# One unread fp32 product of 256 columns on TensorE in every part of an attention step that leaves the shared bank unused

## What is computed

```
q_h = exp_map(split(x @ W_q.T)); k_h = exp_map(split(x @ W_k.T)); v_h = exp_map(split(x @ W_v.T))
dist = arccosh(max(1 + 2c * |q - k|^2 / ((1 - c|q|^2) * (1 - c|k|^2)), 1 + EPS)) / sqrt(c)
weights = softmax(-beta * dist - bias)
x = x + (log_map(exp_map(weights @ v_tan)) joined) @ W_o.T
x = x + fp8_gemm(layernorm(x), kernel) + bias
```

## Time and profile before

| | |
|---|---|
| median of 3 runs | 2432.06 us (2428.98 to 2432.98) |
| the profiled execution | 2433.24 us |
| its span, first to last instruction | 2431.4 us |
| ScalarE busy | 1937.7 us, 80% |
| TensorE busy, matmuls | 1945.1 us, 80% |
| VectorE, GpSimd busy | 970.8 us, 362.6 us |
| mean granted TensorE clock | 0.809 of 2.4 GHz |

### The profile page before, as it was taken

How to read it: one execution, slowest core, us unless ns; L and a number is a source line. 1 busy time by engine, 2 the same in 40 slices (tenths; PEclk the granted TensorE clock), 3 DMA queues, 4 the chain that set the end, 5 groups by cost and what they waited for, 6 DMA issues and landing times. The chain is left out here.

```text
span 2431.4 us, 29241 instructions
## 1 busy us (share of the span) xinstructions
PE 1945.1 (80%) x10317; PEld 624.6 (26%) x10317; DVE 970.8 (40%) x2289; ACT 1937.7 (80%) x1184; POOL 362.6 (15%) x223
## 2 busy tenths in 40 slices
PE   4458897989888768888879489798979888888682
PEld 2222232323222222222323123232323222222221
DVE  4432344343534345343444534443343534221413
ACT  1039999998989659998989389899988989999491
POOL 1111121121212002020212102121121212010011
PEclk9959798988888778897989579898888888876675
DMA  1120101001010200202020020201001010200000
GB/s 37 57 57 10 49 10 51 25 19 58 18 58 1 66 9 11 65 1 75 1 66 10 1 75 1 66 10 66 10 18 58 18 49 1 66 1 18 1 18 10
DMA packets 79154, 75.58 MB, mean 31 GB/s; under 512 B 34651, under 2 KB 60508, under 8 KB 78940
## 3 DMA queue, kind: packets, MB, share of 16 engines
q1 hardware_dynamic: 78940, 73.02, 9.6%
HBM read 17.96 MB, written 55.05 MB: 30 GB/s over the span
## 5 line engine op out<-in xcount | busy, mean ns | idle before, releaser
L911 ACT ACTIVATE U<-ps 128x2048 f32<-128x2048 f32 x500 | 939.0, 1878 | 178.6 <-PE ps L820 169.3
L916 ACT ACTIVATE U<-U,sc 128x2048 f32<-128x2048 f32 x512 | 1025.4, 2003 | 0.0
L820 PE MATMUL ps<-q_T,k_T 18*128 18x512 f32 x4096 | 750.4, 770 | 222.7 <-ACT U L911 149.2
L833 PE MATMUL ps<-U,vals 128*32 128x512 f32 x4096 | 680.6, 743 | 50.1 <-ACT U L916 29.1
L820 PEld LDWEIGHTS ps<-q_T,k_T 18*128 18x128 f32 x4096 | 224.5, 218 | 756.0 <-ACT U L911 592.5
L340 PE MATMUL ps<-wT,xnT 128*128 128x384 f32 x512 | 231.7, 581 | 13.7 <-DVE qkv L370 9.4
L370 DVE COPY qkv<-ps 128x384 f32<-128x384 f32 x128 | 71.4, 558 | 342.4 <-PE ps L340 334.8
L306 POOL TENSOR_TENSOR sqr<-qkv 128x768 f32<-128x768 f32 x64 | 94.1, 1470 | 732.4 <-DVE qkv L370 651.2
L833 PEld LDWEIGHTS ps<-U,vals 128*32 128x32 f32 x4096 | 87.9, 118 | 327.7 <-ACT U L916 216.6
L348 PE MATMUL ps<-ident,rows 128*128 128x128 f32 x512 | 99.2, 325 | 84.6 <-POOL rows L323 66.6
L340 PEld LDWEIGHTS ps<-wT,xnT 128*128 128x128 f32 x512 | 98.3, 213 | 161.5 <-issue 107.2
(11 more groups left out here) (174 smaller groups left out, 1336.3 us busy)
## 6 DMA issues: line engine op xcount, KB each, us to landing
q_scratch<-q_T SPq DMA_DIRECT2D x16, 1024.0 KB, 4.5
k_scratch<-k_T SPq DMA_DIRECT2D x16, 1024.0 KB, 6.9
v_scratch<-vals SPq DMA_DIRECT2D x16, 768.0 KB, 10.9
xt<-in_L_attn_x_dram SPq DMA_DIRECT2D x16, 512.0 KB, 3.8
fi_xt<-in_L_attn_x_dram SPq DMA_DIRECT2D x16, 512.0 KB, 4.7
out_dram<-fi_x SPq DMA_DIRECT2D x16, 512.0 KB, 3.2
rk_scratch<-rk SPq DMA_DIRECT2D x16, 32.0 KB, 12.2
wraw<-in_L_attn_W_q_dram SPq DMA_DIRECT2D x1, 256.0 KB, 2.9
```

The lines of the kernel that those rows point to most:

```text
L820: ins = pe.matmul(g.ps[:, 2 * pair + i, :], a.k_T[HB * h:HB * h + RD, b % 2, hg, kt * P:(kt + 1) * P], a.q_T[HB * h:HB * h + RD, G % 3, hg ...
L833: ins = pe.matmul(g.ps[HB * h:HB * h + VW, 6, :], a.vals[:, b % 2, kt, (hg * HPG + h) // 2, DH * (h % 2):DH * (h % 2) + VW], U[:, n % RING ...
L911: act.activation(U[:, n % RING].rearrange("p b n -> p (b n)"), chunk(n), ACT.Ln, scale=-2.0 / EPS, bias=1.0).then_inc(ln_done, 1)
L916: act.activation(U[:, n % RING], U[:, n % RING], ACT.Exp, scale=g.NEGB).then_inc(exp_done, 1)
```

## The change

The step is written as a loop over its two halves. A half without a use of the shared bank now issues `keep_busy`: a wait until VectorE has copied out all uses so far, and one fp32 product of the identity (stationary) with 256 columns of `woT`, into bank 7. Nothing reads it, it raises no semaphore, and the next use overwrites it. There are 576 such halves among 1024: 121 of half 0 and 455 of half 1.

```diff
+                def keep_busy(used):
+
+                    pe.wait_ge(a.b7_copied, used)
+                    pe.matmul(g.ps[:, 7, 0:D], g.ident[:, :], g.woT[:, 0, :], start=True, stop=True)
+
...
                 for n in range(N):
                     G, s = n // STEPS, n % STEPS
+                    used = first_use[n]
                     if n % UNIT == 0:
                         spread_rq(n)
                     if n + 1 < N:
                         distances(n + 1, 1)
                     distances(n + 2, 0)
-                    for key in in_step(G, s, 0):
-                        use(*key)
-                    if n >= 1:
-                        values(n - 1)
-                    for key in in_step(G, s, 1):
-                        use(*key)
+                    for half in range(2):
+                        if half and n >= 1:
+                            values(n - 1)
+                        keys = in_step(G, s, half)
+                        for key in keys:
+                            use(*key)
+                        used += len(keys)
+                        if not keys:
+                            keep_busy(used)
```

## The result

The changed kernel took 2479.86 us (median of 4 runs, 2471.71 to 2487.69), the kernel before 2430.55 us beside it (2428.98 to 2432.98): ratio 1.020, 95% interval 1.0175 to 1.0226. The change makes the kernel 2% slower. I had forecast 2423 us, range 2370 to 2465 us; sign and range were both wrong.

The account below looks back on a forecast made before the run. TensorE at half clock (38% of the span) sets 4.05 us steps, otherwise ScalarE 3.65 us. Plain steps -12.4 us, thirteen groups +3 us: -9 us on 2433.2, 2424, by the runs' median 2423 us; range 2370 to 2465 us.

Parts of the forecast that it names:

- The prediction's sum for a group with both blocks: Groups 1 to 13: 120.4 + 4.9 + 4.2 + 4.3 - 0.8 = 133.0 us, against 132.8 us before.
- the waits: Behind M7 the product waits for VectorE's late copy; TensorE stands for 1.0 us a group.
- the low clock behind R0: After R0 the clock falls and saturated work runs at half speed: 2.5 us a block.
- The price of the product: One added product costs 0.48 us at full clock, like one of W's four; bounds 0.25 and 0.74 us.
- rival D: The product costs 0.74 us, adding 0.26 us in 11 saturated halves of 14 groups: 2463 us; chance 5%.
- Plain steps: Steps without a use: products fit TensorE's pauses, clock holds at 1.0; groups 14 and 15 gain 12.4 us together.
- M and W steps: "Sum 4.9 us, where nothing is lost today.": Per group: M steps 3.0 us, W steps 1.7 us, less 0.8 us, plus 1.0 us waiting behind M7.
- The two blocks: Around X0 and R0: lateness 1.7 and 1.8 us, low clock 2.5 us each; X 4.2 us, R 4.3 us.
- "I expect about 6 us at 0.5": Behind X0 and R0 the low-clock stretch lasts about 6 us, less than the 10.3 us shown before.
- rival C: Low stretches behind the blocks last as long as before: +56 us, 2479 us; chance 20%, in part or whole.
- Small activations: ScalarE's small work in a group: 120.4 us busy against 116.8 us, less 0.8 us under TensorE's overrun.
- Rival B: The clock holds through the blocks, saving 65 us: 2358 us, or 2390 us in one kind only; chance 20%.

Follow-up runs that it names:

- run 9: run 5 with three more products ahead of Q0 in step 19; 2296.82 us, ratio 0.9446.
- run 12: run 5 with the free-step product only in the first part, ahead of values; 2303.82 us, ratio 0.9462.
- run 1: The changed kernel with product and wait only in steps where neither half uses the shared bank; 2370.15 us, ratio 0.973 to the kernel before.
- run 8: The changed kernel with all its waits, but the product only in steps where neither half has a use; 2416.48 us, ratio 0.9927 to the kernel before.
- run 4: The changed kernel with four more products directly ahead of X0 and six ahead of R0; 2415.08 us, ratio 0.9924 to the kernel before.
- run 7: The changed kernel's waits without any product, and none in the second part of a unit's last step; 2475.14 us, ratio 1.0185 to the kernel before.
- run 5: The changed kernel with products only in free steps, plus four ahead of X0 and six ahead of R0; 2317.13 us, ratio 0.9534 to the kernel before.

## Why the prediction was wrong

The prediction's sum for a group with both blocks was 16.2 us over 116.8 (133.0 us). The eleven groups show 20.95 us. Two terms failed in the main: the waits, which were put at 1.0 us for M7 alone and cost 3.0 us, and the low clock behind R0, which was put at 2.5 us and cost 4.2 us. The parts in turn:

- **The price of the product** was given as 0.48 us, one fourth of W. It is 0.63 us between values and distances; 0.48 us is what it takes within a run of its like (0.47 us in run 9). Between distances and a use it is 0.54 us. The bounds, 0.25 and 0.74 us, held it, and rival D had the right direction. In free steps it is free at the high clock, as predicted (in a low stretch it is not, run 12).
- **Plain steps** were right. Group 14: 120.38 us against 119.1 predicted; the first eleven steps of group 15 fell from 44.5 us to 40.7, 3.8 us against 3.9 predicted, and from step 15 on the gain was 62.3 - 59.95 = 2.3 us against 1.7 (before, the Ln of step 15 starts at 2307.3 us, 0.2 us ahead of the window of the earlier trace rows). The open unit between them lost 1.2 us. The clock there was 1.00, as announced (0.94 at the end).
- **M and W steps: "Sum 4.9 us, where nothing is lost today."** This failed, by its second half. Measured is 7.50 - 1.03 = 6.5 us a group. The products make 3.5 of it (runs 1, 8 and the change), where I had 3.0 + 1.7 - 0.8 = 3.9. That these are near is luck in part: at the 0.63 us that a product takes there, the same sum gives 5.4 us, and where the other 1.9 us went was not traced. The waits make 3.0 us, where I had 1.0, for M7 alone. That wait was read rightly (the distance at step 17 is 4.9 us, "about 5 us" was announced). I had counted a wait as free wherever the copy is over by the time that TensorE has run out of work. It is not free at the start of a unit: the queue must read a flag and branch before it can issue the next distances, and it used to do so under the values.
- **The two blocks** were to cost 4.2 and 4.3 us. Run 4 parts them. X: 4.72 us in steps 3 to 6, less 0.4 us of a small activation, is 4.3 us; 1.9 us of it are the low clock (I had 2.5) and 2.4 us the lateness (1.7). R: 6.3 us, of which 4.2 us are the low clock (2.5) and 2.1 us the lateness (1.8). "I expect about 6 us at 0.5" failed behind R0: it lasts 10.2 us, as before the change. There rival C was right; behind X0, with 3.4 us in most groups, it was not.
- **Small activations**, 2.8 us in my sum: with the clock at 1.00 the steps away from the two blocks still show 0.84 + 0.44 + 1.03 + 1.27 + 0.29 = 3.9 us (run 9). ScalarE's own work is 119.59 - 116.8 = 2.8 us of it, as taken; the other 1.1 us are idle time of ScalarE around it, which the sum left out.

The misses are 1.6 + 0.1 + 2.0 + 1.1 = 4.8 us a group, and they are the whole difference of 20.95 - 16.2. Over the thirteen groups 3 us were forecast and 54.9 + 6.9 = 61.8 us are found; groups 0, 14 and 15 were to win 12.4 us and won 9.8 us. Together that leads from the -9 us forecast to the 52 us found between the first Ln and the last. The largest parts are the waits (2.0 us a group too low) and the R block's low clock (1.7 us); the second had a chance of 20% as rival C, the first was no rival at all. Rival C named 2479 us, within 1 us of what was measured. That is luck: it holds behind R0 only, which is a third of the miss, and behind X0 the low stretch was shorter in seven of eleven groups, as forecast. The mean clock (0.901, "0.88 or more") was predicted well and said nothing on the time: the kernel of run 7 has 0.778 and the changed kernel 0.901, and they take nearly the same.

**The rule on idle gaps.** Rival B was weighed by it. The Trainium skill, "TensorE: Matmul & The Clock Gate", section "Why this matters for your kernels", has idle gaps between bursts lower the clock, and names longer ones than stand here. For the pauses of 1.9 to 2.8 us ahead of X0, R0 and behind Q0 the runs agree in kind and not in length: these shorter pauses were enough, and filled, the clock stays at 1.00 (all eleven groups in run 4, nine in run 9). For plain steps I had read the rule as denying what the trace shows, since the pauses are of 0.65 and 0.70 us only. There too the clock rose to 1.00 once both were filled, so the rule's advice held where my reading of it did not. It says nothing of what a wait in the queue costs.

## What to carry to other kernels

Work that is there to keep the clock up is worth having where the engine has a pause, and only there: the same edit brought 63 us in the free steps and took 110 us in the full ones. Put it ahead of a stall that is known (a late operand), and ahead of an instruction that has the same wait, not behind one whose result is still being read: there its wait holds the queue. Where the clock is low all the same, each further product costs about twice as much (run 12 against run 5). A wait can cost more than the time until its semaphore comes: count what lies behind it in the queue, branches and loads above all, since the queue can no longer run ahead through them; and test the wait without the work, since it may be the larger half.

## What the runs showed of the hardware

- A wait that is over before the engine runs dry still cost 1.1 us at a branch: distances 2.09 us after the values instead of 1.00, listed as "1.02 <-issue". The time from the end of VectorE's read to the distances is the same with the product and without it, 1648.96 - 1647.61 = 1.35 us and 1.29 us, so it is the wait and the branch, not the engine's work. The Trainium skill, "Perfetto Trace Analysis", section "Sequencer Loop", says that a sequencer pushes engine instructions into a queue and executes control instructions itself; the sequencer's records agree, as the load and the branch start only behind the wait (with the waits alone the load at 1650.77 us, the read's end at 1650.58 us).
- One fp32 product of 256 columns costs 0.63 us between values and distances, 0.54 us between distances and a use (fp32 and bf16 uses alike) and 0.47 us in a run. At 1.2 GHz it costs 1.15 us between values and distances.
- A pause of 2.3 us was followed by 3.4 us at 1.2 GHz in most groups and one of 2.8 us by 10.2 us in all, although TensorE was busy without a pause behind both. The length of the pause alone does not set that of the stretch: ahead of X0 it was 2.27 us also in the four groups with 10.2 us.
- Two fp32 products, each in its pause, held the clock at 1.00 in group 14. One of them, or two in bf16, gave 0.92 to 0.97.
